# A fused decoder block on one core: half 0's normalised rows ahead of the shared weights' copies, its shared silu built from tanh, and a second pair of experts ahead of the weights' transposes

## The reference, cut to what matters

```python
x = x + tanh(g_xattn[0]) * L0_xattn(layernorm(x), ctx)   # softmax(LN(p @ kv @ kv.T))
x = x + tanh(g_ffn[0])   * L0_ffn(layernorm(x))          # 32 masked ternary experts, top 1
x = x + tanh(g_xattn[1]) * L1_xattn(ctx, layernorm(x))   # (1-g)*adj + g*sigmoid(sim) where sim is in its row's top 76
x = x + tanh(g_ffn[1])   * L1_ffn(layernorm(x))          # 64 experts, top 8, and one shared expert

# L1_ffn, for each expert and for the shared one
gu = x @ gu_w.T ; inter = silu(gate) * up * W ; out += inter @ dp_w
```

## Time and profile before

| | us |
|---|---|
| median of 3 runs | 391.35 (390.76 to 392.14) |
| the profiled execution | 393.36 |
| its span, first to last instruction | 391.6 |
| TensorE busy | 356.0 (91% of the span) |
| VectorE / ScalarE / GpSimd busy | 271.8 / 179.1 / 162.9 |

### The profile page before, as it was taken

One profiled execution on the slowest core, in us unless ns is written; L12 is line 12 of the kernel. 1 busy time (PEld: TensorE's weight loads), 2 busy tenths in 40 slices (PEclk: granted clock), 3 DMA queues, 4 the chain that ended last, 5 costly groups with the idle time before them and its releaser, 6 DMA issues. The chain is left out here.

```text
span 391.6 us, 7679 instructions
## 1 busy us (share of the span) xinstructions
PE 356.0 (91%) x2407; PEld 218.3 (56%) x2407; DVE 271.8 (69%) x708; ACT 179.1 (46%) x359; POOL 162.9 (42%) x184
## 2 busy tenths in 40 slices
PE   8899849439787999999899999999999999999996
PEld 3676318338342556555457566565656565656564
DVE  4949998899993677987995575657645454545554
ACT  4266928737335446546354545642332323232331
POOL 6924636546272589997669776220000000000000
PEclk9959887959996999999999999999999999999999
DMA  7899949679233333445445451023221221222211
GB/s 189 122 257 218 213 141 327 209 226 303 82 110 113 124 116 135 158 157 179 135 153 171 150 175 65 19 67 121 83 67 67 68 66 65 69 67 67 78 55 54
DMA packets 50346, 51.31 MB, mean 131 GB/s; under 512 B 6732, under 2 KB 41484, under 8 KB 50318
## 3 DMA queue, kind: packets, MB, share of 16 engines
q1 hardware_dynamic: 34430, 38.08, 31.3%
q0 software_dynamic: 9216, 6.29, 9.5%
q10 hardware_dynamic: 6672, 6.59, 5.2%
HBM read 44.13 MB, written 7.08 MB: 131 GB/s over the span
## 5 line engine op out<-in xcount | busy, mean ns | idle before, releaser
L1063 PE MATMUL bank<-early,gu 128*128 128x512 f16 x768 | 178.3, 382 | 2.0 <-DVE arena L1649 2.0
L1063 PEld LDWEIGHTS bank<-early,gu 128*128 128x128 f16 (+1 forms) x768 | 75.3, 99 | 82.8 <-issue 6.0
L507 ACT ACTIVATE arena<-arena 128x512 f16<-128x512 f32 (+1 forms) x66 | 41.6, 630 | 138.3 <-DVE arena L1665 138.3
L1090 PE MATMUL bank<-dp,arena 128*128 128x256 f16 (+1 forms) x768 | 94.2, 273 | 1.1 <-POOL arena L466 0.6
L1090 PEld LDWEIGHTS bank<-dp,arena 128*128 128x128 f16 x768 | 74.4, 98 | 24.2 <-POOL arena L466 4.2
L1649 DVE TENSOR_TENSOR arena<-arena,bank 128x512 f32<-128x512 f32 x64 | 43.8, 684 | 52.9 <-PE bank L1063 30.3
L466 POOL TENSOR_TENSOR arena<-arena 128x512 f16<-128x512 f32 (+1 forms) x33 | 38.3, 1161 | 45.0 <-ACT arena L507 45.0
L1665 DVE TENSOR_TENSOR arena<-arena,early 128x512 f32<-128x512 f32 x64 | 49.8, 779 | 7.9 <-DVE arena L1649 2.7
L757 ACT ACTIVATE arena<-bank 128x512 f32<-128x512 f32 (+1 forms) x66 | 38.7, 587 | 14.9 <-PE bank L1063 14.9
L1675 DVE TENSOR_TENSOR arena<-arena 128x512 f16<-128x512 f32 (+1 forms) x33 | 22.9, 693 | 25.3 <-ACT arena L507 25.3
L407 POOL TENSOR_TENSOR gu<-stage,gu 128x512 f16<-128x512 f32 x32 | 39.1, 1223 | 1.3 <-ACT dp L507 1.3
(11 more groups left out here) (187 smaller groups left out, 367.7 us busy)
## 6 DMA issues: line engine op xcount, KB each, us to landing
early<-token_weights SPq DMA_DIRECT2D x126, 128.0 KB, 2.9
stage<-in_gu_t SPq DMA_DIRECT2D x32, 256.0 KB, 2.7
gu<-in_masks_t POOLq DMA_DIRECT2D x16, 256.0 KB, 24.2
stage<-in_dp_t SPq DMA_DIRECT2D x32, 128.0 KB, 2.6
expert_rows<-arena ACTq DMA_DIRECT2D x12, 256.0 KB
dp<-gu SPq DMA_DIRECT2D x22, 128.0 KB, 3.5
routed_rows<-arena SPq DMA_DIRECT2D x1, 1536.0 KB, 18.0
arena<-routed_rows ACTq DMA_DIRECT2D x3, 512.0 KB, 5.7
```

The lines of the kernel that those rows point to most:

```text
L507: return nc.scalar.activation(dst, src, ACT.Copy, scale=scale)
L1063: last = mm(dst[:, :], w, x16[:, h, b, c, :], start=(k == 0), stop=(k == 3 * C - 1))
L1090: last = mm(dst, inter16[0:m, s, a, k * P:(k + 1) * P], w, start=(q is None and j == 0 and k % 2 == 0), stop=True, skip_group_check=True)
```

## The change

It takes 10 edits together. The transfers of `wk` and `b_k` go from SP's queue to ScalarE's. On ScalarE `scale_rows(0)` goes ahead of `x_rows(2)` and `x_rows(3)`, and the shared expert's two weight copies behind `softmax_rows(0)`; all four `weigh_rows` of half 0 go ahead of `expert_rows(1, 0)`; `high_half(6)` and `(7)` go ahead of the third layer's preparation; `silu_step(0)` computes `tanh(0.5 g)` instead of silu, ahead of `top_rows(0)`, and `silu_step(1)` goes ahead of `prep_weights(0)`. On VectorE `gate_step(0)` turns that into silu with one more instruction (`(tanh + 1) * g`, times half of up) and goes ahead of `top_weigh(0)`; `mask_weights(1)` goes behind the first half's assignment; 7 of the search's steps are done earlier. On POOL `low_half(4)` and `(5)` go ahead of and behind `add_rows`. On TensorE the `symmetric` calls come later among half 1's experts, and the second pair goes ahead of the weights' transposes, which get 3 `keep_busy` matmuls behind them.

```diff
--- before
+++ after
@@ -288,4 +288,2 @@
 
-            sp.dma_start(wk_sb[0:DC, :], wk_t).then_inc(attn_in, 16)
-            sp.dma_start(wk_sb[DC:DC + 1, :], b_k.rearrange("(a d) -> a d", a=1)).then_inc(attn_in, 16)
             for b in range(B):
@@ -482,2 +480,3 @@
             gather(0)
+            low_half(4)
             pool.wait_ge(late_in, 16 * 4)
@@ -485,2 +484,3 @@
                 add_rows(t)
+            low_half(5)
             rsqrt(4, HT)
@@ -488,4 +488,2 @@
             gather(1)
-            low_half(4)
-            low_half(5)
             low_step(0, 1, I1)
@@ -509,2 +507,4 @@
             act.dma_start(ctx_sb[0:DC, :], ctx_t).then_inc(ctx_in, 16)
+            act.dma_start(wk_sb[0:DC, :], wk_t).then_inc(attn_in, 16)
+            act.dma_start(wk_sb[DC:DC + 1, :], b_k.rearrange("(a d) -> a d", a=1)).then_inc(attn_in, 16)
             act.dma_start(wqk_sb[:, 0:DC], wq1_t).then_inc(qk_in, 16)
@@ -595,9 +595,9 @@
             nc.scalar.activation(tg[:, 4:5], gates[:, 4:5], ACT.Tanh, scale=0.5).then_inc(gates_done, 1)
-            act.wait_ge(small_in, 16 * 3)
-            copy(shared16[:, 0, :, :], shared_stage).then_inc(shared_hi, 1)
-            copy(shared_dn16[:, 0, :], shared_dn_stage).then_inc(shared_hi, 1)
+            scale_rows(0)
             x_rows(2)
             x_rows(3)
-            scale_rows(0)
             softmax_rows(0)
+            act.wait_ge(small_in, 16 * 3)
+            copy(shared16[:, 0, :, :], shared_stage).then_inc(shared_hi, 1)
+            copy(shared_dn16[:, 0, :], shared_dn_stage).then_inc(shared_hi, 1)
             qk_rows(1)
@@ -701,5 +701,4 @@
             routed_rows(1, 1)
-            weigh_rows(0, 1)
+            weigh_rows(0, 1, 2, 3)
             expert_rows(1, 0)
-            weigh_rows(2, 3)
             routed_rows(1, 2)
@@ -720,2 +719,4 @@
             store_rows(1, 5)
+            high_half(6)
+            high_half(7)
 
@@ -755,3 +756,6 @@
                 if m == I1:
-                    copy(up_sh[:, :], ps_gate[s][I1:P, :]).then_inc(up_copied, 1)
+                    copy(up_sh[:, :], ps_gate[s][I1:P, :], 1.0 if n else 0.5).then_inc(up_copied, 1)
+                if isinstance(n, int) and n == 0:
+                    nc.scalar.activation(silu[0:m, s, :], ps_gate[s][0:m, :], ACT.Tanh, scale=0.5).then_inc(silu_ready, 1)
+                    return
                 nc.scalar.activation(silu[0:m, s, :], ps_gate[s][0:m, :], ACT.Silu).then_inc(silu_ready, 1)
@@ -765,6 +769,6 @@
             prep_rows(0)
-            top_rows(0)
             silu_step(0, 1, I1)
-            prep_weights(0)
+            top_rows(0)
             silu_step(1, 0)
+            prep_weights(0)
             high_step(0, 1, I1)
@@ -777,3 +781,3 @@
                 high_step(n, s)
-                if n < PAIRS - 4:
+                if 4 <= n < PAIRS - 4:
                     high_half(n + 4)
@@ -1151,3 +1155,2 @@
             routed_x(1, 1)
-            symmetric(0, 0)
             experts(1, 0)
@@ -1155,5 +1158,5 @@
             experts(1, 1)
-            symmetric(0, 1, 0)
             routed_x(1, 3)
             experts(1, 2)
+            symmetric(0, 0)
             routed_x(1, 4)
@@ -1161,2 +1164,3 @@
             routed_x(1, 5)
+            symmetric(0, 1, 0)
             experts(1, 4)
@@ -1172,7 +1176,7 @@
             pair_step(0, 0, 0)
+            pair_step(0, 0, 1)
             prep_wt(0)
+            keep_busy(3, bank[0][:, :])
             first_weights(0, I1)
             first_weights(1)
-            pair_step(0, 0, 1)
-            down(0, 1, None, I1)
             for n in range(3, NS):
@@ -1182,2 +1186,4 @@
                     prep_wt(1)
+                if n == 3:
+                    down(0, 1, None, I1)
                 if n == 27:
@@ -1574,4 +1580,3 @@
             dve.wait_ge(gates_done, 1)
-            mask_weights(1)
-            find(2)
+            find(4)
             attend(0)
@@ -1588,3 +1593,3 @@
             similarity_rows(1)
-            for m in range(2, MB):
+            for m in range(1, MB):
                 mask_weights(m)
@@ -1594,5 +1599,5 @@
             attended(1)
-            find(7)
+            find(10)
             choose(1)
-            find(2)
+            find(4)
             assign_spares(1)
@@ -1640,3 +1645,2 @@
             top_find(0)
-            top_weigh(0)
 
@@ -1647,2 +1651,6 @@
                     dve.wait_ge(up_copied, n // NS + 1)
+                if isinstance(n, int) and n == 0:
+                    half = steps(v.scalar_tensor_tensor(silu[0:m, s, :], silu[0:m, s, :], 1.0, ps_gate[s][0:m, :],
+                                                        ALU.add, ALU.mult))
+                    steps.need(half)
                 up = up_sh[:, :] if m == I1 else ps_up[s][:, :]
@@ -1687,2 +1695,3 @@
             gate_step(0, 1, I1)
+            top_weigh(0)
             gate_step(1, 0)
@@ -1693,3 +1702,3 @@
                 gate_up(n, s)
-                find(4 if n in (2, 3, 4) else 3 if n < 14 else 5)
+                find(3 if 7 <= n < 14 else 4)
                 if 7 <= n < 7 + HT:
```

More of the change, by code:

```diff
@@ L595, in _ @@
             nc.scalar.activation(tg[:, 4:5], gates[:, 4:5], ACT.Tanh, scale=0.5).then_inc(gates_done, 1)
+            scale_rows(0)
+            x_rows(2)
+            x_rows(3)
+            softmax_rows(0)
             act.wait_ge(small_in, 16 * 3)
```

7 lines of the change are left out of this document (2 added, 5 removed).

## The result

Over 20 runs each the median is 391.6 us for the changed kernel and 390.77 for the kernel before, but the ratio is 0.9877 with a 95% interval of 0.9838 to 0.9916: faster by 1.2%. One sentence is needed to read that: every ratio in this document compares only the executions within 1.5% of their kernel's fastest, which are five of the changed kernel's twenty (384.3 to 389.7 us, the profiled one of 390.76 not among them) and nineteen of the kernel before's. The medians over all twenty show no gain. Lines are up to 14 higher than before: a pair is L1067, a down L1094, similar L854, routed_x L972, the gate's product L1657.

The account below looks back on a forecast made before the run. TensorE's matmuls bound the loop; before it, a chain through all engines leaves TensorE waiting or at half clock. Terms -6.4 - 2.9 + 0.2 - 0.8 = -9.9 gave 381.4 us against median 391.35; range 379.3 to 384, all cases to 386.5.

Parts of the forecast that it names:

- the forecast's own case: First attention: TensorE keeps full clock at 18.6 us; 381.4 us, own range 379.3 to 384, chance 0.6.
- the rival in which the clock falls at 18.6 as before: First attention: router's weights no sooner, or the shorter wait still suffices; 385.3 us, from 384.3 to 386.5, chance 0.25.
- term 3: Half 1's routing: choose(1) and slots later, partly offset by VectorE asking for rstd sooner; +0.2 us, ends -1.0 and +1.5.
- term 1: Run-up to the pair loop: second pair fills TensorE's waits, half clock goes; -6.4 us, ends 4.5 and 6.7.
- term 4: In the pair loop: fewer VectorE search steps remove some TensorE waits; -0.8 us, ends 0 and 1.3.
- term 2: First attention: shorter router wait, clock kept, earlier scaling bring choose(0) sooner; -2.9 us, between 1.5 and 4.2.
- Cost nothing as long as their weights are there: high_half(6) and (7) would lie in ScalarE's gap of 5.6 us ahead of prep_rows(0), at no cost.
- TensorE waits 1.37 us at 17.58 for the router's weights: First attention: clock halves at 18.6 in the old profile; the change would shrink the wait to 0 to 0.4 us.
- clock kept at 18.6, falls in the 1.9 us of waiting: First attention, ahead of similar(2): choose(0) gains only 1.5 us; 382.8 us, chance 0.25 of the forecast's 0.6.
- about 5.6: Start of TensorE's work: b_k on ScalarE's queue lands at this us, making TensorE's start 0.4 us later.
- Against that: Half 1's routing: seven earlier search steps and add_rows without its wait let VectorE ask for rstd 1.7 us sooner.
- some 3.7 us in all: Pair loop: TensorE's waits at step 17 (1.37 us) and four other steps, against a cadence of 3.9.

Follow-up runs that it names:

- c12_again: The changed kernel unaltered, timed and profiled once more as the twelfth run: median 389.68 us, ratio 0.9872; profiled execution 388.38 us.
- run 4: The kernel before with the run-up edits alone, first attention, routing and finds as before: 387.11 us, ratio 0.9896.
- run 11: The changed kernel with keys on SyncE's queue and half 0's shared gate as before (Silu, top_weigh(0) ahead of the gates): 391.41 us, ratio 1.0009.
- run 9: The changed kernel with keys on SyncE's queue, low halves back behind gather(1) and high halves back in the loop: 387.91 us, ratio 0.9939.
- run 1: The changed kernel with only the transfers of wk and b_k back on SyncE's queue: 385.48 us, ratio 0.9889.
- run 6: The changed kernel with keys on SyncE's queue and low_half(4), low_half(5) back behind gather(1): 399.32 us, ratio 1.0207.
- run 8: The changed kernel with keys on SyncE's queue and the loop's finds as before: 388.59 us, ratio 0.9921.
- run 10: run 7's kernel with eight matmuls on ones added ahead of similar(2): 387.53 us, ratio 0.9918.
- run 3: The kernel before with only the transfers of wk and b_k moved to ScalarE's queue: 392.71 us, ratio 1.0011.
- run 2: The changed kernel, keys still on ScalarE's queue, with 16 instead of 10 keep_busy matmuls ahead of the keys: 386.33 us, ratio 0.9881.
- run 7: The changed kernel with keys on SyncE's queue and half 1's routing as before (mask_weights(1) first; 2, 7, 2 finds): 386.34 us, ratio 0.9851.
- run 5: The kernel before with only scale_rows(0) and half 0's softmax moved ahead of the shared weights' copies on ScalarE: 391.22 us, ratio 0.9997.

## Why the prediction was right in sign and too large in size

Faster was right: 0.9877 of 391.35 is 386.5 us, at the very end of the range of all cases, where 381.4 was forecast; the gain is half of what was summed. The clock was kept at 18.6, the forecast's own case, and still its range of 379.3 to 384 does not hold the time. That the wider range does is luck: its upper end, 386.5, came from the rival in which the clock falls at 18.6 as before, and no profile of the changed kernel shows that. Every sign of being right that the prediction named came true in c12_again (full clock from 18 to 22, scale_rows(0) at 21.17, choose(0) at 35.38, the pairs 0.30 us apart, 0.17 for the small instruction), and the time was wrong all the same. Of the 4.9 us by which the profiles miss the sum, term 3 holds 3.0, term 1 0.7, term 4 0.65 and term 2 0.5; but term 2 looks good only beside the one execution that it was read from.

- **Term 1 (-6.4) was right in its mechanism**, measured -5.7 in the profile; run 4 has it alone, -4.1 us by its ratio, since the loop's finds, left as before, take 1.6 us back there (259.65 us for 258.07). The wait of 0.30 us for the gate, the TENSOR_SCALAR back at 0.17, the hidden table load and the full clock all came as written. The 0.7 us missed are spread: 1.96 us for first_weights where 1.7 was taken, 0.85 for the three matmuls on ones for 0.64, and 0.1 to 0.2 at a pair or a down. Two things behind it were seen only in runs: with half 0's gate as before nothing is left (run 11), and the long small instruction costs 1.3 us (runs 9 and 1). "Cost nothing as long as their weights are there", said of high_half(6) and (7), hangs on low_half(4): 12 us otherwise (run 6).
- **Term 2 (-2.9) failed.** The step was "TensorE waits 1.37 us at 17.58 for the router's weights" and the clock falls behind it, taken as the kernel's habit, while the sum went against the median. Of the ten profiles with the keys on SyncE's queue six have no such wait; the others have 1.37 (before), 0.39, 0.60 and 2.23 us (runs 6, 8, 10), and the clock fell behind it in two, before and run 10. None of the four with the keys on ScalarE's queue has it, so the move may well help, where there is something to help. How many executions of the kernel before have the wait was not counted. Take it away and little is left of the term: from router_mean's start to choose(0) the old order takes 18.0 us (runs 3, 4), the new one 18.2 to 18.4 where the clock fell ahead of similar(2) (c12_again, runs 1, 2, 7, 9, 11), 17.2 and 17.3 where it held (the result's profile, run 8), and 18.3 in run 6, where it held but VectorE came late. That is 0.8 us better at best, against the 1.5 to 4.2 of the prediction. scale_rows(0) came at 21.17 for the 21.0 forecast, and that did not help: TensorE, 1.0 us later by x_rows, sets the pace.
- **The rival "clock kept at 18.6, falls in the 1.9 us of waiting"** is what c12_again and runs 1, 2, 5, 7, 9 and 11 show, but its figure of 382.8 is still 3.7 us under the result. Runs 6 and 8 kept the clock over the same 1.92 us. In c12_again the granted clock stays at 1.00 through the idle window at 22 and is 0.80 at 24. The profiled execution of the result kept it at this place too: between eight transposes and similar(2) the wait was 1.92, and the matmuls behind took 3.72.

```profile
27.24 1.09 PE L835 MATMUL bank<-ident,X 128*128 128x128 f32 x8
30.25 3.72 PE L854 MATMUL bank<-arena,early 128*128 128x256 f32 x16 [1.92 <-ACT early L505]
```

  A transpose does not count as busy for the clock as a matmul does (the Trainium skill, TensorE: Matmul & The Clock Gate, Part 4: PE-mode transpose): seven of the ten profiles with this wait agree, these rows and runs 6 and 8 do not, so the rule alone does not decide this place.
- **b_k "about 5.6"** was sized wrong: issued at 2.06, it landed at 6.1 (6.8 in the result's own profile), so some 4.0 to 4.7 us where the 3.4 of the wqk row had been taken; why it took longer was not isolated. By the ratio it cost nothing (runs 1 and 3), by the medians it may (run 12).
- **Term 3 (+0.2) was half right, and is the largest miss between the two profiles, +3.2.** The first part came as "1.4" and "1.2" had it: from choose(0) to routed_x(1, 0) the profiles with the change's finds take 48.4 to 48.5 us in runs 1, 2, 9 and c12_again, those with the finds of before 46.6 to 47.5 (before, runs 3, 4, 5), +1.4. (The others with the change's finds have 47.4 in the result's, 48.2 in runs 6 and 11, 50.3 in run 8; with the old ones it is 47.7 in run 7, 45.5 in run 10.) The step that failed is "Against that", the 1.7 us by which VectorE asks sooner for rstd: from routed_x(1, 0) to the first pair it is 27.9 to 29.0 us with the change and 28.3 to 29.0 with the finds of before, so nothing comes back (run 6, with its stall, left aside). In c12_again and run 2 it is 30.5 and 30.6: these two lose the clock behind the wait for ScalarE, and that was no term at all. That wait, 1.5 to 3.2 us, is in every profile with four weigh_rows ahead of expert_rows(1, 0) but run 1's, where weigh_rows finds its rows fetched; at the same place run 8 waited 1.74 us and kept the clock. No run took the weigh_rows or the symmetric calls back, so what these two edits are worth is open. Run 7's ratio leans against the new finds too, 1.5 us better than run 1, but the intervals overlap.
- **Term 4 (-0.8) came out at -0.15**, inside its ends. It started from "some 3.7 us in all" of waiting; the idle times of before's loop add up to 2.98. The waits of 0.60 and 0.18 us went as said, but 0.69 at 149.04 came and 0.43 became 0.73: TensorE reaches these steps 5 us sooner, VectorE does not. Left as they were, the finds would have given 1.7 us of the run-up back (run 8), so this edit earns its place although the stretch hardly changed.

The cause of the gain, then, is the run-up. Everything ahead of it brings nothing or costs: the first pair starts at 110.3 to 112.1 us in runs 3, 4 and 5, with the old order or one edit and the router in time, and at 111.6 to 114.5 in c12_again and runs 1, 2, 8 and 9. No version is clearly faster than the changed kernel: run 7's 0.9851 is the lowest ratio, and its interval overlaps that of 0.9877. It was not repeated.

## What to carry to other kernels

A stall seen in one profile is a term only if other executions have it: a gain reckoned from a stall of that execution must not be taken off the median of all, and signs that are read against that profile can all come true while the gain does not. When an edit fills a wait, ask what new wait it opens behind itself (here four weigh_rows that wait for fetched rows) and whether TensorE's clock survives that one. Before moving an instruction ahead in an in-order queue, follow what it waits for to the end of the chain, here ScalarE's copy, SyncE's load, GpSimd's release of the stage; two moves that look apart can be one. And where an early stage gets faster, reckon again what is paced to it: work spread over a loop to fit the old start no longer fits the new one.

## What was not expected of the hardware

- A wait of 1.92 us at the same place, with the same instructions around it, left the clock at full in some executions (similar(2) in 3.72 us: the result's profile, runs 6 and 8) and at half in others (5.2 to 5.4: c12_again, runs 1, 2, 5, 7, 9, 11). The new wait in half 1's experts does the same: behind 1.93 us the clock fell in c12_again, behind 2.23 us in run 9 it held at 1.00.
- In the profile of run 7 the window from 3 to 23 us shows a granted clock of 1.00 throughout (after POOL's bracket), and yet the 16 matmuls of similar take 6.45 us where others need 3.72. The profile of run 11 has the same (6.42 us). The clock's row doesn't explain it, and with it the cause stays open (the executions took 393.43 and 398.90 us):

```profile
3.00:23.00 20.00, 20.00 (x43) 10.65 (x41) 11.41 (x39) 7.09 (x16) 13.33 (x23) 1.00 0.90 186
```

```profile
18.63 6.45 PE L854 MATMUL bank<-arena,early 128*128 128x256 f32 x16
```

- A VectorE instruction of 128x4 beside GpSimd's halving took 1.93 us and ended with the second of its two instructions (114.05 and 114.02 in run 9), as the earlier trace rows had suggested; alone it took 0.17.
